# Layer 3's experts: the first four tiles' rows picked by products with ones, and gates and places in another order

## The reference, cut to what matters

```python
x = x + _L3_attn_ref(_layernorm(x), ...)
x = x + _L3_xattn_ref(_layernorm(x), ctx_1024, W, b)   # two 128x128 products and a bias
x = x + _L3_ffn_ref(_layernorm(x), wg_red, wg, w1, b1, w2, b2)

def _L3_ffn_ref(hidden_states, wg_red, wg, w1, b1, w2, b2):
    x = hidden_states.reshape(-1, c)
    logits = (x @ wg_red.T) @ wg_unit.T                 # 8 experts
    gates = softmax(logits); indices_s = argmax(gates); scores = max(gates)
    for e in range(8):
        mask = (indices_s == e)[:, None]
        h = gelu(x @ w1[e] + b1[e])                     # 128 -> 512
        out = out + mask * (h @ w2[e] + b2[e])          # 512 -> 128
    return (out * scores[:, None]).reshape(b, t, c)
```

## Time and the profile before

| | us |
|---|---|
| timed runs, median of 3 | 1227.04 (1226.87 to 1227.51) |
| profiled execution | 1221.58 |
| its span on the core | 1219.8 |
| mean granted PE clock in it | 0.898 of full |
| PE busy | 968.9 (79%) |
| DVE busy | 746.4 (61%) |
| ACT busy | 615.5 (50%) |
| POOL busy | 397.2 (33%) |

### The profile page before, as it was taken

One profiled execution on the slowest core, in us unless ns is written; L12 is line 12 of the kernel. 1 busy time (PEld: TensorE's weight loads), 2 busy tenths in 40 slices (PEclk: granted clock), 3 DMA queues, 4 the chain that ended last, 5 costly groups with the idle time before them and its releaser, 6 DMA issues. The chain is left out here.

```text
span 1219.8 us, 21732 instructions
## 1 busy us (share of the span) xinstructions
PE 968.9 (79%) x7938; PEld 720.2 (59%) x7938; DVE 746.4 (61%) x1793; ACT 615.5 (50%) x1615; POOL 397.2 (33%) x498
## 2 busy tenths in 40 slices
PE   6448787784988787798998998999878995288587
PEld 4325455453975355577995775676546884144487
DVE  4788886793523766734236664766577776776433
ACT  1138775572645546745645775677403222376144
POOL 3178772673223124500002332333420003111234
PEclk9679988997998888989999999999978998598579
DMA  7900000004464000020000000000203000000171
GB/s 247 194 4 1 1 1 19 1 2 125 134 179 173 1 1 2 2 104 1 1 1 1 2 1 1 2 1 1 117 2 138 1 1 17 0 1 2 42 223 49
DMA packets 49977, 54.83 MB, mean 45 GB/s; under 512 B 12280, under 2 KB 41328, under 8 KB 48560
## 3 DMA queue, kind: packets, MB, share of 16 engines
q1 hardware_dynamic: 47760, 48.84, 13.4%
q0 software_dynamic: 2112, 4.60, 1.1%
HBM read 43.04 MB, written 10.91 MB: 44 GB/s over the span
## 5 line engine op out<-in xcount | busy, mean ns | idle before, releaser
L315 POOL TENSOR_TENSOR norm_rstd<-norm_std,minus_half 128x4 f32<-128x4 f32 x24 | 25.5, 1062 | 296.2 <-DVE norm_std L310 296.1
L2615 POOL TENSOR_TENSOR arena<-arena 128x512 f32<-128x512 f32 x64 | 66.7, 1042 | 150.0 <-DVE arena L2664 150.0
L2604 ACT ACTIVATE arena<-arena 128x128 f32<-128x128 f32 x256 | 99.2, 391 | 19.9 <-DVE arena L2631 19.9
L1321 ACT ACTIVATE arena<-bank,w_L_ffn_b1T 128x512 f32<-128x512 f32 x64 | 43.2, 689 | 53.0 <-PE bank L1263 52.7
L2627 DVE SCALAR_TENSOR_TENSOR arena<-bank,bufA 128x512 f32<-128x512 f32 x64 | 43.8, 685 | 35.2 <-PE bank L2553 35.2
L1263 PE MATMUL bank<-x_high,w_low 128*128 128x512 f32 x136 | 58.6, 431 | 4.9 <-DVE w_low L1272 4.8
L1298 PEld LDWEIGHTS bank<-bufB,arena 128*128 128x128 f32 x512 | 59.4, 192 | 1.1
L1298 PE MATMUL bank<-bufB,arena 128*128 128x128 f32 x512 | 59.8, 275 | 0.0
L1583 ACT ACTIVATE arena<-bank,w_L_ffn_b1T 128x128 f32<-128x128 f32 x128 | 36.4, 370 | 41.1 <-PE bank L1572 41.1
L542 PE MATMUL bank<-arena 128*128 128x512 f32 x64 | 38.5, 694 | 21.9 <-DVE arena L502 18.9
L1263 PE MATMUL bank<-x_low,w_high 128*128 128x512 f32 x136 | 55.0, 404 | 0.0
(11 more groups left out here) (527 smaller groups left out, 2764.3 us busy)
## 6 DMA issues: line engine op xcount, KB each, us to landing
bufB<-in_L_ffn_w SPq DMA_DIRECT2D x28, 256.0 KB, 2.9
bufA<-in_L_ffn_w SPq DMA_DIRECT2D x2, 2048.0 KB, 10.0
bufB<-in_L_ffn_W SPq DMA_DIRECT2D x2, 2048.0 KB, 11.0
bufB<-in_L_ffn_w SPq DMA_DIRECT2D x2, 2048.0 KB, 9.9
arena<-in_L_ffn_w SPq DMA_DIRECT2D x12, 256.0 KB, 2.9
rows_one<-blank SPq DMA_DIRECT2D x4, 704.0 KB, 12.4
bufA<-in_L_ffn_Wgu SPq DMA_DIRECT2D x1, 2304.0 KB, 8.9
bufA<-in_L_attn_Wqkv SPq DMA_DIRECT2D x1, 2048.0 KB, 7.7
```

What stands on the lines that cost most here:

```text
L1321: act.activation(m["h"][k % 2][:, f, :], banks[f][:, :], ACT.Gelu, bias=b1[:, c:c + 1]).then_inc(g["hidden"].sem, 1)
L2604: o = act.activation(tile, tile, ACT.Exp, bias=b2["mn"][n % 8][:, j:j + 1], scale=-1.0, accum_out=b2["sm"][n % 8][:, j:j + 1])
L2615: pool.tensor_tensor(tile, tile, bc(b2["rs"][n % 4], 2, P), ALU.mult).then_inc(g["over_sum"].sem, 1)
```

## The change

**Half 0's routing is moved ahead.** PE makes half 0's logits and counts before it turns half 1 for the cross step. DVE ranks half 0 before it centres half 1; ACT makes half 0's exponential before it copies half 1.

**Tiles 0 to 3 are picked.** DVE compares a row of the numbers 0 to 511 ("count") with each token's place and gets four 128x512 blocks of ones and zeros (picks_dve); PE multiplies the four blocks of normed rows by them and sums in bank 0 (tiles_pick_pe), which gives the four turned tiles at once. rows0 of half 0 is no longer loaded. The scatter and the other loads stay.

**Half 1's routing goes into the tile loop.** PE turns half 1 after tile 0's up product, makes its logits at the end of step 1 and its counts at the end of step 2. DVE does all of half 1's routing, from the statistics to the owners, after it has copied the first group in, and before result 0. ACT copies half 1 after tile 0's gelu.

**Gate.** Half 1's exponential is made by POOL as e to the power v, 32 columns (gate_exp_one_pool). ACT calls a gelu on one column before the tile loop.

**Small parts.** rows_rest is split into tiles 0 to 3 and 4 to 10, and so is the copy of the places; half 1's loads wait for the first group's copy, since its rows lie where the picks do. The banks of the results of tiles 0 to 5 are 5 and 6 in turn; half 1's routing uses bank 7. A memset of "euler" is added at the start, an iota of 512 columns at POOL's unit 4 of the attention.

```diff
-                         (blkneg, 0.0), (anyblk, 1.0), ..., (route["one"], 1.0)):
+                         (blkneg, 0.0), (anyblk, 1.0), ..., (route["one"], 1.0),
+                         (euler, float(np.e))):
...
+        def picks_dve(dve, e):
+            for b in range(4):
+                dve.tensor_scalar(e["picks"][b], e["count"], route["m"][:, 0, b:b + 1], None,
+                                  ALU.is_equal).then_inc(e["g"]["picks"].sem, 1)
+
+        def tiles_pick_pe(pe, e):
+            for b in range(4):
+                pe.wait_ge(*e["g"]["picks"](b + 1))
+                o = pe.matmul(banks[0][:, :], e["sent"][0][:, b, 0:P], e["picks"][b], start=b == 0, stop=b == 3)
+            o.then_inc(e["g"]["tiles_turned"].sem, 1)
...
         def layer3_cross_pe(pe):
             turn_x_pe(pe, "L3_ffn", 0, 1, e3["sent"][0])
-            turn_x_pe(pe, "L3_xattn", 1, 6)
             pe.wait_ge(*norm["L3_ffn"]["xn0"](1))
             route_logits_pe(pe, e3, 0, gate_w3[:, :], 4)
             route_counts_pe(pe, e3, 0, 4)
+            turn_x_pe(pe, "L3_xattn", 1, 6)
             mix_pe(pe, 1, 5)
...
         def layer3_cross_dve(dve):
             stats_dve(dve, "L3_xattn", 1)
+            route_one_dve(dve, 0, 4)
             centre_dve(dve, "L3_xattn", 1)
-            route_one_dve(dve, 0, 4)
             gate_one_dve(dve, 0)
             route_slots_dve(dve, e3, 0, 4)
+            picks_dve(dve, e3)
             mix_add_dve(dve, 1, 5)
...
+        RESULT_BANKS = [5 + n % 2 if n < 6 else (7, 5, 6)[n % 3] for n in range(2 * one.n)]
...
+        def gate_exp_one_pool(pool, h):
+            pool.wait_ge(*e3["g"]["gate_low"](h + 1))
+            v = route["v"][:, :, :]
+            pool.tensor_tensor(v, euler[:, :].rearrange("p (b n) -> p b n", n=NE), v, ALU.pow).then_inc(e3["g"]["gate_exp"].sem, 1)
...
+            if h:
+                sync.wait_ge(*g["tiles_in"](1))
+            for n, a, b, f in (("rows0", 0, 4, slice(0, P)), ("rows1", 4, 8, slice(0, P)), ("rows_rest", 0, 4, slice(P, ROW)),
+                               ("rows2", 8, one.n, slice(0, P)), ("rows_rest1", 4, one.n, slice(P, ROW))):
+                if n == "rows0":
+                    if h:
+                        sync.dma_start(e3["rows"][h][:, a:b, f], rows[:, a:b, f]).then_inc(g[n].sem, 16)
+                    continue
...
         def layer3_experts_pe(pe):
-            turn_x_pe(pe, "L3_ffn", 1, 7, e3["sent"][1])
-            pe.wait_ge(*norm["L3_ffn"]["xn1"](1))
-            route_logits_pe(pe, e3, 1, gate_w3[:, :], 7)
-            route_counts_pe(pe, e3, 1, 7)
             pe.wait_ge(*in_B(80))
-            tiles_pe(pe, e3)
+
+            def ahead(pe, n):
+                if n == 0:
+                    turn_x_pe(pe, "L3_ffn", 1, 7, e3["sent"][1])
+                if n == 1:
+                    pe.wait_ge(*norm["L3_ffn"]["xn1"](1))
+                    route_logits_pe(pe, e3, 1, gate_w3[:, :], 7)
+                if n == 2:
+                    route_counts_pe(pe, e3, 1, 7)
+
+            tiles_pe(pe, e3, ahead)
...
         def layer3_experts_act(act):
-            keep_xnT(act, "A", "L3_ffn", 1, 7)
-            gate_exp_one_act(act, 1)
+
+            act.activation(gmx[:, 0:1], gmx[:, 0:1], ACT.Gelu)
             act.wait_ge(*weights("L3_ffn"))
-            tiles_act(act, e3)
...
         def layer3_experts_pool(pool):
             scatter_one_pool(pool, 0)
             rstd_pool(pool, "L3_ffn", 1)
+            gate_exp_one_pool(pool, 1)
             scatter_one_pool(pool, 1)
             results_one_pool(pool)
 
         def layer3_experts_dve(dve):
-            stats_dve(dve, "L3_ffn", 1)
-            centre_dve(dve, "L3_ffn", 1, e3["sent"][1])
-            route_one_dve(dve, 1, 7)
-            gate_one_dve(dve, 1)
-            route_slots_dve(dve, e3, 1, 7)
-            tiles_dve(dve, e3, lambda n: result_one_dve(dve, n))
+            def ahead(dve, n):
+                if n == 0:
+                    stats_dve(dve, "L3_ffn", 1)
+                    centre_dve(dve, "L3_ffn", 1, e3["sent"][1])
+                    route_one_dve(dve, 1, 7)
+                    gate_one_dve(dve, 1)
+                    route_slots_dve(dve, e3, 1, 7)
+
+            tiles_dve(dve, e3, lambda n: result_one_dve(dve, n), ahead)
```

More of the change, by code:

```diff
@@ L213, in build_program @@
         blank = sb("blank", [P, P])
+        euler = sb("euler", [P, 4 * NE])
         numbers, unsent = sb("numbers", [P, 4]), sb("unsent", [P, TILES_ONE, 2])
@@ L3389, in build_program @@
+        e3 = dict(st="L3_ffn", k=1, plan=one, neighbours=1, rows=[in_bufA(one.n, ROW), in_low(one.n, ROW)])
+        e3["picks"], e3["count"] = [in_high(BANK) for _ in range(4)], in_bufA(BANK)
         e3["sent"], e3_b2 = [in_bufA(4, ROW) for _ in range(2)], in_bufA(NE * P)
-        e3["in"], e3["hidden"] = [in_bufA(BANK) for _ in range(2)], [e3_late(FF // P, P) for _ in range(3)]
-        e3["out"] = [e3_late(P) for _ in range(2 * one.n)]
-        e3["extra_tiles"] = [(e3_late(FF), e3_late(FF), e3_late(FF // P), e3_late(P)) for _ in range(2 * (one.n - NE))]
@@ L3393, in build_program @@
-        assert 2 * one.n * (ROW + P) // 2 + 3 * FF + 2 * (one.n - NE) * (2 * FF + FF // P + P) <= 15200
+        e3["in"], e3["hidden"] = [in_bufA(BANK) for _ in range(2)], [in_low(FF // P, P) for _ in range(3)]
+        e3["out"] = [in_low(P) for _ in range(2 * one.n)]
+        e3["extra_tiles"] = [(in_low(FF), in_low(FF), in_low(FF // P), in_low(P)) for _ in range(2 * (one.n - NE))]
+        assert one.n * (ROW + 2 * P) + 3 * FF + 2 * (one.n - NE) * (2 * FF + FF // P + P) <= 15200
         e3["extra"] = [signal(f"extra{i}", 128) for i in range(one.n - NE)]
-        e3["g"] = {**sparse_signals(one, 1), **{n: signal(n, total) for n, total in (
-            ("kept_tokens", 2), ("rows_rest", 32), ("results", 2 * one.n))}}
+        e3["g"] = {**sparse_signals(one, 1, 16), **{n: signal(n, total) for n, total in (
+            ("kept_tokens", 2), ("picks", 4), ("rows_rest", 32), ("rows_rest1", 32), ("results", 2 * one.n))}}
@@ L3398, in build_program, with e3_result @@
         returned = [signal(n, 16 * one.n) for n in ("returned", "gathered")]
-        e3["result"] = lambda n: (banks[5 + n % 3][:, 0:P], e3["g"]["results"](n - 2) if n >= 3 else
-                                  e3["g"]["slots"](2) if n == 2 else None)
+        RESULT_BANKS = [5 + n % 2 if n < 6 else (7, 5, 6)[n % 3] for n in range(2 * one.n)]
+        def e3_result(n):
+            last = max((k for k in range(n) if RESULT_BANKS[k] == RESULT_BANKS[n]), default=None)
+            free = e3["g"]["slots"](2) if n == 6 else e3["g"]["results"](last + 1) if last is not None else None
+            return banks[RESULT_BANKS[n]][:, 0:P], free
@@ L3401, in build_program @@
+        e3["result"] = e3_result
         places = sb("places", [P, 2, one.n], U32)
@@ L3476, in rows_one_load @@
             rows = rows3_d[h].rearrange("(n p) f -> p n f", p=P)
-            for n, a, b, f in (("rows0", 0, 4, slice(0, P)), ("rows1", 4, 8, slice(0, P)), ("rows_rest", 0, one.n, slice(P, ROW)),
-                               ("rows2", 8, one.n, slice(0, P))):
+            if h:
[3 more added lines that the diff above has]
+                if n == "rows0":
+                    if h:
+                        sync.dma_start(e3["rows"][h][:, a:b, f], rows[:, a:b, f]).then_inc(g[n].sem, 16)
+                    continue
                 if h:
@@ L3486, in result_one_dve @@
             o, row = e3["out"][n], e3["rows"][h]
-            if i == 0:
-                dve.wait_ge(*g["rows_rest"](16 * (h + 1)))
-                dve.tensor_copy(places[:, h, :], row[:, :, 2 * P]).then_inc(*dve_step.next())
+            if i in (0, 4):
+                a, b = (4, one.n) if i else (0, 4)
+                dve.wait_ge(*g["rows_rest1" if i else "rows_rest"](16 * (h + 1)))
+                dve.tensor_copy(places[:, h, a:b], row[:, a:b, 2 * P]).then_inc(*dve_step.next())
             dve.wait_ge(*g["down_made"](n + 1))
```

26 lines of the change are left out of this document (17 added, 9 removed).

## The result

Twenty executions of the changed kernel have a median of 1229.3 us (1225.06 to 1234.99), twenty of the kernel before 1225.62 us (1221.58 to 1232.65); the first four of these are the four of the table ahead of the prediction. The ratio is 1.0032 with a 95% interval of 1.0018 to 1.0047: the change costs 3.7 us where 5.8 us less were predicted, and the time lies outside the range, on the other side of no change. The profiled execution took 1225.87 us, with a span of 1224.1.

The account below looks back on a forecast made before the run. No engine bounds the whole span; only the last 85 us can change, where PE waits. Gain 9.7 at full clock, less 1.7 and 2.0 for clock falls and 0.2 for the power: 5.8 off 1227.04, 1221.2 us; range 1217.3 to 1225.6.

Parts of the forecast that it names:

- POOL's result scatters queue behind half 1's [...] and catch up by tile 14: Result scatters on POOL wait until 1171, then take 1.26 us each against 1.79 a tile; no charge.
- After it nothing differs, so the end moves as it moves: After tile 4's up, at 1177.13 before, both kernels run alike, so its shift is the shift of the end.
- The power: Half 1's exponential on POOL, 32 columns: taken as 2.7 us against 2.5 us of cover, 0.2 lost.
- rival 2: Power priced per column, 7.1 us; DVE waits some 4.4 beyond the cover; gain 1.4 to 2, 1225.3; chance 0.15.
- a sign of being wrong: Prediction wrong if the power exceeds 5 us, PE waits for half 1's rows before tile 9, or x sum passes 1148.4.
- the x sum 0.7 earlier: Half 1's x sum: with half 0's routing ahead, the mixing product ends at 1147.6, so the sum comes 0.7 earlier.
- products with ones 3.5 to 5 us: PE's eight 512-column instructions picking tiles 0 to 3, from 1147.6: 3.5 to 5 us.
- tile 0's up 22.4 us behind the x sum: Tile 0's up product on PE starts at 1152.8, 12.5 us before the old 1165.26.
- centring 25.0: Half 1's centring on DVE at 1155.4 in place of 1153.87, 1.5 later, behind the first group's copy.
- the clock at 0.50 after both pauses: PE's clock falls to half twice for 3 to 5 us between 1156 and 1174, losing 1.7 and 2.0 us.
- Tile 4's up, forecast 5.8 earlier: The one mark for the gain: tile 4's up on PE near 1171 against 1177.13.
- tile 0's head start: Tile 0 no longer stands behind half 1's routing, giving 9.7 us up to tile 4's up at full clock.

Follow-up runs that it names:

- session 3: Changed kernel a fourth time, unchanged, against the kernel before on chip 14: ratio 1.0021 (0.9996-1.0046), 91.41 us from half 0's x sum to the end.
- sessions 1 and 2: Changed kernel repeated unchanged, a second and third time, against the kernel before on chips 9 and 8: ratios 0.9961 and 0.9970.
- six stores fewer: Results-between kernel without the indirect stores of results 0 to 5, second run, against the kernel before: ratio 0.9926, 80.00 us from half 0's x sum to the end.
- session 2: Chip 8, in turn with the kernel before: changed kernel 0.9970, half 0's order only 0.9969, results between 0.9918 (the row of seventeen DMAs).
- session 1: Chip 9, in turn with the kernel before: changed kernel's second run 0.9961, with exponential on ACT 0.9927.
- second, third and first profile: Changed kernel, unchanged each time, against the kernel before: ratios 0.9961, 0.9970 and 1.0032; x sum to end 85.65, 86.24 and 88.20 us.
- results between: Changed kernel with exponential on ACT and DVE doing results 0 and 1 between parts of half 1's routing, against the kernel before: 0.9918, 0.9992, 1.0000.
- exponential on ACT: Changed kernel with half 1's exponential back on ACT in place of the power on POOL, against the kernel before: ratios 0.9927 and 0.9998.
- early rows: Results-between kernel with SyncE loading half 0's rows again as half 1's, ahead of half 1's scatters, against the kernel before: ratio 0.9999.

## Why the prediction was wrong

- **The step that failed** is "POOL's result scatters queue behind half 1's [...] and catch up by tile 14", with no charge, and with it "After it nothing differs, so the end moves as it moves". The pile-up was foreseen, its price was not. Half 1's routing stands behind tile 2, so results 0 to 3 come due while its four scatters go out, and POOL issues one unbroken row. In the first result and session 3 PE stood 2.94 and 4.18 us for a gelu behind it; from tile 4's up to the end it took 47.28 and 49.91 us, against 42.67 before. Without holds PE doesn't stand behind the row, yet the stretch is 43.14 and 44.73 us in sessions 1 and 2: the clock was still at half for 1.0 and 4.2 us behind tile 4's up, which is the 0.5 and 2.1 us more. So "after it nothing differs" was wrong by the clock too.
- **How far that reaches**: the profile after is 4.3 us longer than the one before where 5.8 less were forecast. Of these 10.1 us the hold and the clock are 4.6. The other 5.5 lie ahead of half 0's x sum, in code that the change doesn't touch, where the trace after has the holds of layer 0 and the trace before has not. So the sign of the first result isn't shown to come from the change; that its gain is gone where the holds are is shown (1.0021, 0.9996 to 1.0046 in session 3).
- **What is shown of the cause**: each hold lies in or just behind an unbroken row of eight or more; with six stores fewer the one trace that had holds in layer 0 has none at the end, and the ratio is some 0.007 lower than with them in other sessions. A hold doesn't need the loads of half 1's rows. The row alone doesn't bring it (seventeen in a row without one in session 2): it comes only under conditions that are not the kernel's. What these are, whether recording the trace is among them, and how a row of POOL's DMAs delays what ACT and DVE see of PE, stays open. That a row put into the kernel before would bring a hold was only tried under conditions without any.
- **The power** (2.7 us, 0.2 lost) was the mis-sized term: 5.43 us, nearer to rival 2's 7.1, and over the 5 us that the prediction named as a sign of being wrong. DVE took the counts 3.0 us late in session 1 and 1.4 in the first result, where the counts ended at 1170.40 and the power at 1171.45. "GPSIMD Engine Reference" of the Trainium skill (section 3.1) has a two-input operation at some 2.6 cycles per element, under 0.1 us for 28 columns more; the products took 201 ns at 4 columns and 234 at 24, in keeping with it, the power did not.
- **Right, or nearly**, in the second, third and first profile: the x sum 0.7 earlier (0.8, 1.4 and 1.7: it came 17.26, 16.65 and 16.32 us behind half 0's in place of 18.02); products with ones 3.5 to 5 us (4.89 in the second, 3.60 in the first); tile 0's up 22.4 us behind the x sum (22.69, 21.81, 20.51); centring 25.0 (25.20, 24.32, 23.02); the clock at 0.50 after both pauses, but first for 10.3 us (1158.60 to 1168.90) in the first profile and not for 3 to 5, with PE busy 9.58 of it. Tile 4's up, forecast 5.8 earlier, came 4.2, 5.2 and 5.8 earlier. The match in the first profile is in part luck: the power and the longer half clock cost more than charged, so the rest of the stretch took less, and which term of it is not told apart.
- **Where the gain was looked for**: the sum credited tile 0's head start. Half 0's order alone reaches tile 4 at 42.92 us and the end at 85.63; the head start adds nothing to that at the end (85.65 and 86.24), because PE then stands 5.49 us for result 0. The prediction named that wait ("for which PE stands") and didn't ask what the change would be without it. With results between and the exponential on ACT, the same head start is worth 5 us (85.63 to 80.26).

In sessions 1 and 2 the medians, 4.9 and 3.1 us below the kernel before, come near the forecast of 5.8, but by half 0's order and not by the head start that the sum credited, so that is partly luck. In session 3 and in the first result the hold and the clock take the gain back.

## To carry to other kernels

Count the indirect DMAs that POOL will issue without a pause once work is moved earlier, and keep such rows short: a queue that catches up cost PE nothing in the sessions without holds and 3 to 9 us in the others. Measure by a mark behind the last shared instruction and again at the end, in more than one session and with both kernels' traces from the same one, before a sign is believed for a change of 0.3%. When a routing step goes between tiles, look at once at what stands behind it on the in-order engine: here two results that could have gone first were worth as much as the whole change.

## What the runs showed of the hardware

- With POOL's indirect DMAs 0.30 us apart for eight or more, ACT and DVE can take PE's finished products 3.5 us (first result, 1182.82 to 1186.35) to 9.3 us (early rows, 1171.55 to 1180.81) late, with waits named "remote"; in another session on the same chip they did not, and in session 2 not in a row of seventeen. "SBUF — State Buffer" of the Trainium skill (section "SBUF: two separate sides") says that PE and ACT never wait on anyone at SBUF's engine ports; this case's trace has ACT idle 5.89 us, the last 4.8 of them behind a product that ended at 322.25, so if that rule holds the delay lies elsewhere.
- A power on POOL costs 0.40 us and 0.157 us a column of 128 partitions, a product 0.20 us at 4 columns and 0.23 at 24.
